# Joining a projection with its windowed attention, and moving the last expert gatings from VectorE to GpSimd

## What is computed

```
q, k, v = split(shift_token(x) @ wqkv, 3)
q, k = rotary_xpos(l2norm(q) * qs, l2norm(k) * ksc)
x = x + local_attention(q, k, v) @ wo          # then a gated hidden layer
```

```
scores = softmax(x @ Wr + br)                  # 2048 x 64
# per expert sort the tokens by score, sum in groups of 64, keep the
# 512 best of the 2048 group sums; the mask goes back to the tokens
fs = kept scores / their sum
h = silu(x @ Wup + bup) * (x @ Wgate + bgate) * fs
out = h @ Wdown + fs @ bdown
```

## Time and profile before

| | before |
|---|---|
| time, median of 3 runs | 1312.14 us (1308.63 to 1313.78) |
| time of the profiled execution | 1312.41 us |
| its span in the trace | 1310.6 us |
| mean granted TensorE clock | 0.942 of full speed |
| engine busy shares | PE 87%, DVE 67%, ACT 45%, POOL 32% |
| stage F1 ends, layer 1 and 2 | at 482.6 and 694.2 us |
| M0's units / its comparisons | 1052.8 to 1179 / 1177.0 to 1202.2 us |

### The profile page before, as it was taken

One profiled execution on the slowest core, in us unless ns is written; L12 is line 12 of the kernel. 1 busy time (PEld: TensorE's weight loads), 2 busy tenths in 40 slices (PEclk: granted clock), 3 DMA queues, 4 the chain that ended last, 5 costly groups with the idle time before them and its releaser, 6 DMA issues. The chain is left out here.

```text
span 1310.6 us, 29016 instructions
## 1 busy us (share of the span) xinstructions
PE 1140.5 (87%) x11396; PEld 689.9 (53%) x11396; DVE 884.6 (67%) x1510; ACT 592.6 (45%) x1392; POOL 425.6 (32%) x376
## 2 busy tenths in 40 slices
PE   6899899899898869999877999877995799974997
PEld 5577655577544448654446854534662454432343
DVE  3777545777456857534884733796665589999687
ACT  2566444666345659533657923402661355520100
POOL 0366401566206965312994530033441000000000
PEclk9899999899999979999997999998997889985999
DMA  3100000200002210011220000000000011100011
GB/s 79 61 15 2 2 13 17 75 2 1 2 1 57 56 29 3 2 67 32 57 52 2 4 15 13 12 4 4 5 5 1 13 22 21 19 6 1 13 31 45
DMA packets 52711, 28.05 MB, mean 21 GB/s; under 512 B 35458, under 2 KB 46188, under 8 KB 52204
## 3 DMA queue, kind: packets, MB, share of 16 engines
q1 hardware_dynamic: 52588, 26.33, 8.2%
HBM read 17.13 MB, written 1.05 MB: 14 GB/s over the span
## 5 line engine op out<-in xcount | busy, mean ns | idle before, releaser
L337 POOL TENSOR_TENSOR A_pr<-A_pr,A_rs 128x1024 f32<-128x1024 f32 x64 | 121.2, 1895 | 66.6 <-DVE A_rs L401 66.6
L391 DVE TENSOR_REDUCE A_mx<-psb 128x1 f32<-128x1024 f32 x64 | 77.8, 1215 | 21.2 <-PE psb L350 21.1
L434 ACT ACTIVATE A_pr<-psb,A_nm 128x1024 f32<-128x1024 f32 x64 | 71.5, 1117 | 22.9 <-DVE A_nm L395 22.6
L1164 POOL TENSOR_TENSOR F_raw<-F_raw,F_rc 128x1024 f32<-128x1024 f32 x32 | 75.6, 2363 | 17.3 <-DVE F_raw L1229 16.9
L361 PE MATMUL psb<-ident,A_pr 128*128 128x128 f32 x512 | 71.6, 284 | 3.1 <-POOL A_pr L337 3.1
L1881 ACT ACTIVATE M_hall<-psb,M_bu 128x512 f32<-128x512 f32 x64 | 44.0, 688 | 61.2 <-PE psb L1823 61.2
L361 PEld LDWEIGHTS psb<-ident,A_pr 128*128 128x128 f32 x512 | 56.2, 144 | 26.1 <-POOL A_pr L337 15.6
L2072 PE MATMUL psb<-M_hb,M_wd 128*128 128x512 f32 x128 | 68.2, 615 | 0.0
L1823 PE MATMUL psb<-XL,M_wu 128*128 128x512 f32 x128 | 66.8, 604 | 1.1 <-ACT M_ST L1890 1.1
L1194 PE MATMUL psb<-ident,F_raw 128*128 128x128 f32 x256 | 38.5, 298 | 33.3 <-POOL F_raw L1167 33.3
L1183 PE MATMUL psb<-F_wqkv,F_hst 128*128 128x512 f32 x128 | 61.6, 604 | 6.4 <-ACT F_hst L1241 4.5
(11 more groups left out here) (347 smaller groups left out, 2916.0 us busy)
## 6 DMA issues: line engine op xcount, KB each, us to landing
F_VS<-F_V SPq DMA_DIRECT2D x62, 128.0 KB, 2.3
F_raw<-in_c_xpos_dram SPq DMA_DIRECT2D x3, 1024.0 KB, 4.8
F_wqkv<-in_L_ffn_wqkv_dram SPq DMA_DIRECT2D x3, 768.0 KB, 7.2
A_w<-in_L_attn_w_dram SPq DMA_DIRECT2D x4, 256.0 KB, 3.3
M_wu<-in_L_ffn_Wup_dram SPq DMA_DIRECT2D x16, 64.0 KB, 2.0
M_wg<-in_L_ffn_Wgate_dram SPq DMA_DIRECT2D x16, 64.0 KB, 2.2
M_wd<-in_L_ffn_Wdown_dram SPq DMA_DIRECT2D x16, 64.0 KB, 1.8
M_sel<-in_c_select_dram SPq DMA_DIRECT2D x16, 64.0 KB, 1.9
```

The source lines that it names most:

```text
L337: pool.tensor_tensor(p, p, rs[:, u % 2:u % 2 + 1].broadcast_to([P, SEQ]), ALU.mult).then_inc(scaled, 1)
L391: dve.tensor_reduce(mx[:, u % 2:u % 2 + 1], sview(u), AX, ALU.max).then_inc(maxed, 1)
L434: act.activation(pr[:, u % NP, :], sview(u), ACT.Exp, bias=nm[:, u % 2:u % 2 + 1], scale=scale, accum_out=su[:, u % 2:u % 2 + 1]).then_inc ...
L1164: pool.tensor_tensor(rs[:, o, :], rs[:, o, :], rc[:, o, :], ALU.add).then_inc(unit, 1)
```

## The change

1. **Join.** `window_attention` takes the projection's programs as a `Stage` (`first`) and runs them at the head of its own, in one block. TensorE does `scores(0)` ahead of `turn(14)` and `scores(1)` ahead of `turn(15)`, each once `rope` and the squares of the tile that held those banks are done. ScalarE does `exp(0)` between `keep(14)` and `keep(15)`. VectorE goes on with `top(0)` right after its last `rope`. Before `scores(2)` TensorE waits for all of q, k, v and the moved v.
2. **Gatings.** The gatings of units 47 to 63 leave VectorE. ScalarE reads the gate product of those units itself, with its bias, into one of 12 SBUF buffers (`late_gate`), and GpSimd multiplies it into `hall`, starting after the first `spread`. Whoever waited for a gating now waits with `wait_read(engine, n)`: for `gated` up to 47, and for ScalarE's `copied` beyond.
3. **Order of the end of M0.** The last 5 units (59 to 63) are made by TensorE inside the comparisons, one after each of iterations 7 to 11, all in banks 0 and 1. The transposes go from the last four tiles to the first, with a semaphore for each four, and the comparisons go from m = 15 down to m = 0, starting after the first four.

```
-                        scores(0)
-                        scores(1)
+                        first.multiply(pe, scores)
...
                             for o in range(2):
+                                pe.wait_ge(squared, NT - 1 + o)
+                                pe.wait_ge(roped, NT - 1 + o)
+                                scores(o)
                                 turn(NT - 2 + o, o, False)
+                            pe.wait_ge(q_kept, NT)
+                            pe.wait_ge(k_kept, NT)
+                            pe.wait_ge(v_kept, NT)
+                            pe.wait_ge(v_moved, 16 * (2 * NT - 1))
...
                             keep(NT - 2)
+                            exp(0)
                             keep(NT - 1)
...
+            TAIL = 5
+            SLOTS = 12
+            FIRST = NU - 17
...
+                        if u >= FIRST:
+                            act.wait_ge(gate_rdy, u + 1)
+                            if u - FIRST >= SLOTS:
+                                act.wait_ge(joined, u - FIRST - SLOTS + 1)
+                            act.activation(late_gate(u), bank[pair_bank[u] + 1], ACT.Identity, bias=bg[:, b % 3:b % 3 + 1]).then_inc(copied, 1)
...
+                    pool.wait_ge(spread, 1)
+                    for u in range(FIRST, NU):
+                        pool.wait_ge(copied, u - FIRST + 1)
+                        pool.tensor_tensor(hall_of(u), hall_of(u), late_gate(u), ALU.mult).then_inc(joined, 1)
...
-                    for u in range(2, NU - 1):
+                    for u in range(2, NU - TAIL):
                         unit(u)
-                    pe.wait_ge(gated, NU - 3)
+                    wait_read(pe, NU - TAIL)
                     pe.wait_ge(summed, 2)
-                    for n in range(NT):
-                        last = pe.transpose(Gb[:, n * P:(n + 1) * P], Gc[:, n:n + 1].broadcast_to([P, P]), ident[:])
-                    last.then_inc(spread, 1)
-                    unit(NU - 1)
+                    for k in reversed(range(NCH)):
+                        for n in range(4 * k, 4 * k + 4):
+                            last = pe.transpose(Gb[:, n * P:(n + 1) * P], Gc[:, n:n + 1].broadcast_to([P, P]), ident[:])
+                        last.then_inc(spread, 1)
...
+                    for i, m in enumerate(reversed(range(NT))):
+                        pe.wait_ge(less, i + 1)
...
+                        if 7 <= i < 7 + TAIL:
+                            unit(NU - TAIL + i - 7)
...
-                    dve.wait_ge(spread, 1)
-                    for m in range(NT):
-                        if m >= 2:
-                            dve.wait_ge(counted, m - 1)
+                    for i, m in enumerate(reversed(range(NT))):
+                        if i % 4 == 0:
+                            dve.wait_ge(spread, i // 4 + 1)
+                        if i >= 2:
+                            dve.wait_ge(counted, i - 1)
...
-                        if m == 0:
-                            unit(NU - 1)
```

More of the change, by code:

```diff
@@ L473, in window_attention, with _ @@
                 with nc.Block() as block:
+                    @block.sync
+                    def _(sp):
+                        first.fetch(sp)
                     @block.gpsimd
                     def _(pool):
+                        first.side(pool)
                         for n in range(NG):
@@ L581, in add @@
                             dve.tensor_tensor(dst[:, cs(c)], dst[:, cs(c)], bank[c], ALU.add).then_inc(added, 1)
+                        first.combine(dve)
                         top(0)
@@ L617, in keep @@
                             act.activation(pt[:, n % 2, 0:4, :], bank[4].rearrange("p (w n) -> p w n", n=P), ACT.Copy).then_inc(kept_a, 1)
-                        exp(0)
+                        first.activate(act, exp)
                         for n in range(NG + 1):
@@ L624, in _ @@
                                 keep(n - 1)
-                clear(g)
+                clear(first.flags + g)
         def local_maxima(tag, Q, KM, masks, ends, first, MT):
@@ L1133, in build @@
                                                 "turned q_kept k_kept dstep v_moved", st)
-                    with ExitStack() as sc, nc.Block() as block:
+                    with ExitStack() as sc:
                         hs = XL
@@ L1142, in build, with fetch @@
                         HT = NT // 2
-                        @block.sync
-                        def _(sp, l=l):
+                        def fetch(sp):
                             issue(sp, loaded, hidden_weights(l))
@@ L1153, in _, with side @@
                             sp.wait_ge(v_moved, 16 * (2 * NT - 1))
-                        @block.gpsimd
-                        def _(pool):
+                        def side(pool):
                             for o in range(2):
@@ L1173, in _, with multiply @@
                                     finish(2 * i + o, o, False)
-                        @block.tensor
-                        def _(pe):
+                        def multiply(pe, scores):
                             def make(n, o, first):
@@ L1236, in _, with activate @@
                                     rope(2 * i + o, o, False)
-                        @block.scalar
-                        def _(act):
+                        def activate(act, exp):
                             def stage(n, o):
@@ L1272, in _ @@
                             keep(NT - 2)
+                            exp(0)
                             keep(NT - 1)
[L1274 to L1278, removed]
+                        window_attention("F2", QT, KT, V, VS, mask, [u.rearrange("p (w n) -> p w n", n=P) for u in (XL[:, 0:2 * CH], XL[:, 2 * CH:T])]
+                                         + [raw[:, o, :, :].rearrange("p s (w n) -> p (s w) n", n=P) for o in range(2)],
+                                         tab[:, :, :, :].rearrange("p o s (w n) -> p o (s w) n", n=P), 8.0,
+                                         [F_wo[:, j, :] for j in range(4)], H,
+                                         Stage(g, fetch, side, multiply, activate, combine))
                 g = loaded, drawn, a_rdy, g_rdy, gelu_rdy, hid_out, sum_rdy, added, tabled = sems(
@@ L1799, in build, with hall_of, late_gate, wait_read @@
                 need = sb("M_need", [P, 8], stack=sa)
+                def hall_of(u):
+                    b, c = divmod(u, NCH)
+                    return hall[:, b * T + c * CH:b * T + (c + 1) * CH]
+                def late_gate(u):
+                    i = u - FIRST
+                    k = i % SLOTS
+                    if k < 4:
+                        return H[:, cs(k)]
+                    return FAB[:, 2, cs(k - 4)] if k < 6 else raw_gates[:, k - 6, :]
+                def wait_read(engine, n):
+                    engine.wait_ge(gated, min(n, FIRST))
+                    if n > FIRST:
+                        engine.wait_ge(copied, n - FIRST)
                 @block.sync
```

36 lines of the change are left out of this document (19 added, 17 removed).

## The result

| | before | after |
|---|---|---|
| time, median of 20 runs each | 1314.03 us (1308.63 to 1321.94) | 1300.88 us (1291.47 to 1310.77) |
| ratio, with its 95% interval | | 0.990 (0.9884 to 0.9916) |
| profiled execution, span, mean clock | 1312.41, 1310.6 us, 0.942 | 1301.93, 1300.2 us, 0.944 |

The change makes the kernel 1.0% faster. 1291.4 was forecast with a range up to 1300: the time lies 9.5 above the value and 0.9 outside the range. A second set of runs of the same kernel gave 1299.34.

A forecast was written before the change was run, and what follows sets the result against it. Latency was taken to bound the join; TensorE the expert stage up to unit 58, then VectorE. Terms -14.6 - 6.2 = -20.8 took the profiled 1312.41 to 1291.6, the median 0.3 lower: 1291.4 us, range 1286 to 1300.

The forecast's parts named there:

- Join, -14.6: Seam of projection and attention: scores(2) starts 7.4 us earlier in the first layer, 7.2 in the second, together -14.6.
- ScalarE did not pause behind the table load: Rival at the join: a pause as long as the load delays exp(0) by 1.3 us per layer, 1294.0; chance 0.05.
- The attention gave nothing back: Rival: slack in the attention's steady state takes back half the join's gain, 1298.7, or all, 1306; chance 0.05.
- Sort, -0.7: Expert stage, sort's half steps: TensorE's 1.72 us a unit sets the pace; L1967 starts at 1157.0 instead of 1157.71.
- ScalarE did not become the bound: Rival in the sort: ScalarE's work exceeds TensorE's 1.72 us, 8 steps slip 0.6 each, 1296.4; chance 0.07.
- To the comparisons: End of M0, from L1967 at 1157.0 to VectorE's first comparison at 1168.7 instead of 1177.00.
- Comparisons: End of M0: 24.5 us of comparing plus 2.8 of stalls; last comparison ends at 1196.0 instead of 1202.22, -6.2.
- the half-clock rival: Comparisons: TensorE stays at half clock through units 59 to 63, +0.9 there, 1298.5 in all; chance 0.12.
- blocking by GpSimd: Rival: GpSimd's 17 multiplications hold VectorE 1.2 us each during the comparisons, about 1312 to 1319; chance 0.04.
- Behind the comparisons nothing is changed: Rest of the kernel after the last comparison: nothing changed, no term in the sum; SP's weight loads only hang on earlier reads.

The follow-up runs named there:

- the padded kernels: Kernel before, and kernel before with the join alone, each with the 64-row products (base term, totals) widened to 128 rows by zeros: 1310.76 and 1296.47 us.
- join_only: The kernel before with the join alone, M0 and its gatings, transposes and comparisons left as before: 1296.29 us, ratio 0.9859.
- m0_only: The kernel before with only the changes to gatings, transposes and comparisons, window_attention left as before: 1309.94 us, ratio 0.9965.
- rows128: The changed kernel with the 64-row products at the seam of M0 and M3 (base term and totals) widened to 128 rows by zeros: 1288.67 us, ratio 0.9811.

## Why the prediction was off

- **Join, -14.6: right.** 3.19 and 3.14 us from the last `turn` to `scores(2)`; forecast were 2.83 (479.52 to 482.35) and 3.0. The prediction's own terms, 481.4 for the end of `exp(0)` and 1.1 for `keep(15)`, make 482.5, not 482.35. From the projection to M0 the four traces of before lie at 652.3 on average and those of after at 636.7, so 15.5; single traces spread over some 4 us here (13.0 in the first pair), and the padded kernels give 14.3 in time. ScalarE did not pause behind the table load (0.02 us). The attention gave nothing back. The Trainium skill (ScalarE: Activation LUTs, What ACT_TABLE_LOAD costs) has a drain of 1.38 us beside the load; no run here shows it on this path.
- **Sort, -0.7: right in sense, small.** 104.6 on average before, 104.0 after. TensorE's 1.72 us a unit keeps its pace; ScalarE did not become the bound: the half steps start 1.71 us apart.
- **To the comparisons: right.** 11.7 forecast (1157.0 to 1168.7), 11.9 measured, 19.3 before.
- **Comparisons: right.** 27.3 us forecast, 27.4 measured (1155.02 to 1182.44). One unit at half clock, stalls of 1.20, 0.80 and 0.40 where 1.4, 0.9 and 0.25 were named. Neither the half-clock rival (all five units) nor blocking by GpSimd is there.
- **"Behind the comparisons nothing is changed": this step failed.** The instructions are the same, and the mask even takes 0.6 us less (16.6 against 17.2), which I had not seen. But the time of the same instructions is not: in three of four traces of the changed kernel M3 takes 9.5 to 10 us more. The terms up to M3's first product sum, by the averages of four traces each, to -15.5 - 0.6 - 7.5 + 2.4 - 0.6 = -21.8; I had -20.8. M3 takes 85.6 on average of the four traces after, against 78.1: with these +7.4 it is -14.4, and with the +9.8 of a trace that has the fall -12.0. The difference of the medians, -13.15, lies between. I had costed the tail at nothing without asking at which level TensorE's clock would enter it, although the comparisons ahead of it, with TensorE mostly idle, were being reordered. My rival of a half clock sat in the wrong place: in units 59 to 63, where five full units lift it, and not behind the products of 64 rows.
- **The range.** It reached to 1300 by that misplaced rival. The fall costs 10 us on top of 1291.4, which is 1301.4, and it stands in 3 of 4 traces; so the median sits there and not at my value. The kernel's own spread (1291.5 to 1310.8 over 20 runs) is in part this, in part the start: the projection begins between 399 and 407 us over all traces, ahead of all that is changed.

**What stays open.** What decides whether the clock falls in an execution, at a seam with the same instructions and the same idle time. The traces show the clock low during the comparisons in both kernels and rising again in the idle products, and the M0 part sets when: in `join_only` it rises 9.20 us ahead of M3's first product as in the four traces of before, in `m0_only` 9.86 as in the changed kernel (9.87 to 10.09). Among the unpadded traces the three with the fall have 9.97, 10.03 and 10.09, and the two of the M0 order without it 9.86 and 9.87. A tenth of a microsecond divides the two kinds, in five traces. No run moved the rise by itself, so this is a pattern, not a cause shown. What is shown is what ends the fall: 128 rows in either group of products; `rows128` has its rise at 10.01 and no fall.

## What to carry to other kernels

"The instructions behind this are unchanged" is not yet "their time is unchanged": where TensorE sets the pace of what follows, look at the granted clock at its start in several executions, not in one. When two edits bring less together than the better one does alone, compare stretch by stretch between fixed marks; the loss is then one number in one column. A product with few rows that takes as long as a full one can be given zero rows for nothing, and here that held the clock.

## What the runs showed of the hardware

- TensorE at 1.2 GHz for some 20 us while busy all the time, with four products of 64 rows (float32, 512 columns) among those of 128; with these widened by zeros 3.4 us, with those ahead of them widened too, none. About 10 us of the kernel's time hang on it.
- The width in rows costs nothing by itself: 3.67 us for four products (eight records) at 64 rows and at 128. With the totals padded too, M3 took 77.0 us against 78.1 without a fall: a chunk with a total of 128 rows among the other products took 1.95 us, one with a total of 64 rows 2.34.
- The same work can meet TensorE's clock at slightly different points: among the four traces of the changed kernel the clock rises 9.97, 10.03 and 10.09 us ahead of M3's first product where the fall follows, and 9.87 where it does not.
